# Layer 1's maximum subtracted by TensorE, a reordered first turn, and a store moved between loads, in a four-layer gated attention kernel

## Time and profile before

| what | value |
| --- | --- |
| median of the runs | 2130.57 us (2121.48, 2130.57, 2133.06) |
| the profiled execution, its own time | 2118.36 us |
| its span | 2116.6 us |
| granted TensorE clock, mean | 0.927 |
| PE busy | 1850.4 us, 87% |
| DVE busy | 1648.8 us, 78% |
| ACT busy | 583.1 us, 28% |
| POOL busy | 655.1 us, 31% |

### The profile page before, as it was taken

One profiled execution on the slowest core, in us unless ns is written; L12 is line 12 of the kernel. 1 busy time (PEld: TensorE's weight loads), 2 busy tenths in 40 slices (PEclk: granted clock), 3 DMA queues, 4 the chain that ended last, 5 costly groups with the idle time before them and its releaser, 6 DMA issues. The chain is left out here.

```text
span 2116.6 us, 37275 instructions
## 1 busy us (share of the span) xinstructions
PE 1850.4 (87%) x14832; PEld 1038.7 (49%) x14832; DVE 1648.8 (78%) x2940; ACT 583.1 (28%) x1331; POOL 655.1 (31%) x786
## 2 busy tenths in 40 slices
PE   8687879888798887988874799999999999999987
PEld 6333455435554355533542355555555555555543
DVE  4489776996669966699655688888888888888895
ACT  3321233212322123222234122222222222222344
POOL 3410223002330023300222543434344444444463
PEclk8899989998799987999877899999999999999998
DMA  8737204362043610446005211111111112111011
GB/s 238 209 122 212 77 2 137 109 191 65 2 141 116 184 60 2 141 120 180 1 1 174 80 51 51 51 51 50 51 51 46 51 35 66 26 46 31 26 41 51
DMA packets 141771, 176.48 MB, mean 83 GB/s; under 512 B 46752, under 2 KB 81728, under 8 KB 141472
## 3 DMA queue, kind: packets, MB, share of 16 engines
q1 hardware_dynamic: 139584, 172.88, 27.6%
q10 hardware_dynamic: 2016, 1.22, 0.3%
HBM read 131.98 MB, written 42.08 MB: 82 GB/s over the span
## 5 line engine op out<-in xcount | busy, mean ns | idle before, releaser
L1266 POOL TENSOR_TENSOR early_vare<-early_mv,w_eps 128x1 f32<-128x1 f32 x96 | 29.7, 309 | 750.2 <-DVE early_mv L1349 741.4
L2404 POOL TENSOR_TENSOR la_q<-la_straight,la_rot 128x512 f32<-128x512 f32 x128 | 163.0, 1274 | 163.7 <-DVE la_rot L2474 163.7
L434 PE MATMUL la_ps<-w_xTh,w_wqh 128*128 128x512 bf16 x512 | 196.2, 383 | 14.4 <-POOLq L116 8.0
L832 PE MATMUL early_ps<-early_products,w_heads 128*32 128x512 f32 x1024 | 140.1, 672 | 63.4 <-DVE early_products L1502 35.9
L435 PE MATMUL la_ps<-w_xTl,w_wqh 128*128 128x512 bf16 x512 | 195.0, 381 | 0.0
L436 PE MATMUL la_ps<-w_xTh,w_wql 128*128 128x512 bf16 x512 | 194.6, 380 | 0.0
L434 PE MATMUL la_ps<-w_woh,la_oTh 128*128 128x512 bf16 x512 | 194.0, 379 | 0.3 <-issue 0.3
L435 PE MATMUL la_ps<-w_wol,la_oTh 128*128 128x512 bf16 x512 | 194.0, 379 | 0.0
L436 PE MATMUL la_ps<-w_woh,la_oTl 128*128 128x512 bf16 x512 | 194.0, 379 | 0.0
L2417 POOL TENSOR_TENSOR la_p<-la_s,la_rec 128x256 f32<-128x256 f32 x128 | 89.9, 703 | 273.3 <-DVE la_rec L2495 273.3
L2336 ACT ACTIVATE la_oTh<-la_ps 128x256 bf16<-128x256 f32 x256 | 84.0, 380 | 293.5 <-PE la_ps L2219 293.5
(11 more groups left out here) (352 smaller groups left out, 4609.4 us busy)
## 6 DMA issues: line engine op xcount, KB each, us to landing
early_vR<-scr_v SPq DMA_DIRECT2D x128, 257.0 KB, 5.2
early_wkv<-wkv SPq DMA_DIRECT2D x32, 512.0 KB, 4.5
la_v<-v SPq DMA_DIRECT2D x64, 256.0 KB, 4.0
k<-early_ctxt SPq DMA_DIRECT2D x32, 256.0 KB, 3.9
v<-early_ctxt SPq DMA_DIRECT2D x64, 128.0 KB, 3.0
scr_p<-early_weights SPq DMA_DIRECT2D x16, 512.0 KB, 2.6
early_pR<-scr_p SPq DMA_DIRECT2D x32, 256.0 KB, 3.5
w_raw_q<-in_Wq SPq DMA_DIRECT2D x8, 1024.0 KB, 7.4
```

Of the source, the lines that this page charges most:

```text
L434: pe.matmul(out, lh[c], rh[c], start=(first and c == 0), stop=False)
L832: last = pe.matmul(out[32 * g:32 * g + 32, :], w["heads"][:, HEADS * (1 - odd):HEADS * (1 - odd) + 32], src(2 * g + odd), start=(opens and ...
L2404: rope_sum.send(pool.tensor_tensor(dst, straight[:, slot, :], rot[:, slot, :], ALU.add))
```

## The change

It has three parts.

1. The subtraction. `shift_scores` becomes `largest`: VectorE takes only the negated maximum. TensorE adds it to the scores in PSUM with a product of the identity and the maximum, repeated 16 times by a stride of zero (`centre`, two products a tile). ScalarE takes the exponential from PSUM into ee, half by half. `largest(3)` stands ahead of `times_values(1)`, and a second group of last-layer keys and values is ahead of the first `sum_depth`.
2. The store. Tile 3's eight value loads are issued four and four, with the store of its weights between.
3. The first turn. The opening's loads and products are in another order, Wq comes in two halves; the splits of the later weights, the signs, POOL's low splits, the stores of layer 1's values and ScalarE's splits 6 and 7 have other places.

```diff
     def load_product(self, sp):
-        sp.dma_start(self.wq[:, :, :], io["L0_Wq"].rearrange("(c p) n -> p c n", p=P)).then_inc(self.loaded, 16)
-        sp.dma_start(self.wk[:, :, :], io["L0_Wk"].rearrange("(c p) n -> p c n", p=P)).then_inc(self.loaded, 16)
-        sp.dma_start(self.bq[:, :], io["L0_bq"]).then_inc(self.loaded, 16)
-        sp.dma_start(self.bk[:, :], io["L0_bk"]).then_inc(self.loaded, 16)
+        sp.dma_start(self.bq[:, :], io["L0_bq"]).then_inc(self.wk_loaded, 16)
+        sp.dma_start(self.bk[:, :], io["L0_bk"]).then_inc(self.wk_loaded, 16)
+        sp.dma_start(self.wk[:, :, :], io["L0_Wk"].rearrange("(c p) n -> p c n", p=P)).then_inc(self.wk_loaded, 16)
+        for h in range(2):
+            cols = slice(2 * h * P, 2 * (h + 1) * P)
+            sp.dma_start(self.wq[:, :, cols], io["L0_Wq"].rearrange("(c p) n -> p c n", p=P)[:, :, cols])\
+              .then_inc(self.wq_loaded[h], 16)
...
     def product(self, pe, banks):
-        pe.wait_ge(self.loaded, 4 * 16)
-        for m in range(C):
-            banks.wait_free(pe, 0, "M", m)
...
+        pe.wait_ge(self.wk_loaded, 3 * 16)
         banks.wait_free(pe, 0, "r")
...
+        banks.wait_free(pe, 0, "s")
...
+        for m in range(C):
+            if m % 2 == 0:
+                pe.wait_ge(self.wq_loaded[m // 2], 16)
+            banks.wait_free(pe, 0, "M", m)
...
         banks.wait_free(pe, 0, "c")
...
-        banks.wait_free(pe, 0, "s")
```

On SP, first turn:

```diff
-                    first_keys_values(0, 1, 2, 3)
+                    first_keys_values(0, 1, 2)
...
                     if j == 1:
-                        for k in range(2):
-                            load_values(sp, turn, k)
+                        if turn == 0:
+                            first_keys_values(3)
+                        else:
+                            for k in range(2):
+                                load_values(sp, turn, k)
                 if turn == 0:
-                    first_keys_values(4, 5, 6, 7)
+                    first_keys_values(4, 5)
+                    load_values(sp, turn, 0)
                     for g in range(2):
+                        first_keys_values(KV - 2 + g)
                         prep.wait_kv_kept(sp, KV - 2 + g)
                         load_kv_weights(turn, g)
+                    load_values(sp, turn, 1)
```

On SP, every turn:

```diff
-                shifted_values(turn, 3)
-                weights_by_shift(turn, 3)
+                banks.wait_filled(sp, turn, "sum1", 1)
+                load_values(sp, turn, 3, range(CH // 2))
+                write_weights(turn, 3)
+                load_values(sp, turn, 3, range(CH // 2, CH))
+                read_weights(turn, 3)
```

On TensorE:

```diff
+                def centre(j):
+                    for h in range(2):
+                        mx1_ready.wait(pe, turn, 2 * j + h)
+                        at = slice(h * (TP // 2), (h + 1) * (TP // 2))
+                        centred.send(pe.matmul(banks.bank("dot1", j, h).rearrange("p (t w) -> p t w", w=WIN), ident,
+                                               mx1[:, at].unsqueeze(2).to_broadcast([P, TP // 2, WIN]),
+                                               start=False, stop=True, skip_group_check=True))
...
                 queries_keys(1)
-                last_keys_values(0)
+                last_keys_values(0, 1)
                 sum_depth(0)
                 queries_keys(2)
-                last_keys_values(1, 2)
+                centre(0)
+                last_keys_values(2)
                 sum_depth(1)
                 queries_keys(3)
+                centre(1)
                 last_keys_values(3, 4, 5)
                 sum_depth(2)
                 last_keys_values(6, 7)
                 sum_window(0)
                 out_proj(0)
+                centre(2)
                 last_keys_values(8, 9)
                 sum_depth(3)
-                last_keys_values(10, 11)
+                last_keys_values(10)
+                centre(3)
+                last_keys_values(11)
                 sum_window(1)
```

On ScalarE:

```diff
             def exponentials1(turn, j):
-                banks.wait_drained(act, turn, "dot1", j, 0)
-                banks.wait_drained(act, turn, "dot1", j, 1)
-                exp1_ready.send(act.activation(ee[:, :, :], ee[:, :, :], ACT.Exp, scale=float(CH) ** -0.5))
+                for h in range(2):
+                    at = slice(h * (TP // 2), (h + 1) * (TP // 2))
+                    if h == 0 and j >= 1:
+                        p1_ready.wait(act, turn, j - 1)
+                    centred.wait(act, turn, 2 * j + h)
+                    banks.drain(act.activation(ee[:, at, :].rearrange("p t w -> p (t w)"), banks.bank("dot1", j, h),
+                                               ACT.Exp, scale=float(CH) ** -0.5), "dot1", j, h)
...
                     aT_high.send(act.activation(aTh[:, j, :, :], aT[:, j % 2, :, :], ACT.Copy))
+                    if turn == 0 and j < 3:
+                        prep.high(act, *(("R1",), ("W1",), ("Wqd", "Wkv", "R3"))[j])
...
                 route_exp(turn, 0, e0, R0)
-                if turn == 0:
-                    prep.split_kv_high(act, 6)
                 hsT_copy(turn, 0)
                 if turn == 0:
-                    prep.split_kv_high(act, 7)
+                    prep.split_kv_high(act, 6, 7)
```

On POOL:

```diff
-                    prep.split_kv_low(pool, 0, 1, 2, 3)
+                    prep.split_kv_low(pool, 0, 1, 2)
+                rstd_of(turn, 1)
+                if turn == 0:
+                    prep.split_kv_low(pool, 3)
                     pool.wait_ge(prep.biased, 1)
-                rstd_of(turn, 1)
                 add_bias(turn, 0, 1)
                 if turn == 0:
-                    prep.split_kv_low(pool, 4, 5, 6, 7)
+                    prep.split_kv_low(pool, 4, 5)
                 rstd_of(turn, 2)
+                if turn == 0:
+                    prep.split_kv_low(pool, 6, 7)
```

On VectorE:

```diff
             def first_turn(j):
-                if j == 0:
+                if j == 1:
                     prep.low(dve, "R1")
-                elif j == 1:
+                elif j == 2:
                     prep.low(dve, "W1")
-                elif j == 2:
+                elif j == 3:
                     prep.low(dve, "Wqd", "Wkv", "R3")
-                else:
-                    prep.below_zero(dve)
-                    prep.signs(dve)
...
                 n = st.step(dve.tensor_scalar(rec[:, :], rec[:, :], w["gates"][:, 0:1], None, ALU.mult))
+                if turn == 0:
+                    prep.below_zero(dve)
+                    prep.signs(dve)
+                    dve.wait_ge(prep.signed, 2)
...
-                def shift_scores(j):
+                def largest(j):
...
-                        st.link(dve.tensor_reduce(mx1[:, at], dots, AX.X, ALU.max))
-                        ins = dve.tensor_tensor(ee[:, at, :], dots,
-                                                mx1[:, at].unsqueeze(2).to_broadcast([P, TP // 2, WIN]), ALU.subtract)
-                        banks.drain(ins, "dot1", j, h)
+                        mx1_ready.send(dve.tensor_reduce(mx1[:, at], dots, AX.X, ALU.max, negate=True))
...
                 times_keys(3)
                 divide(2)
+                largest(3)
                 times_values(1)
-                shift_scores(3)
                 divide(3)
```

More of the change, by code:

```diff
@@ L302, in product @@
         banks.fill(last, "r")
+        banks.wait_free(pe, 0, "s")
+        for c in range(C):
+            last = pe.matmul(banks.bank("s")[:, 0:1], bq[:, c:c + 1].to_broadcast([P, P]), bk[:, c:c + 1],
+                             start=(c == 0), stop=(c == C - 1))
+        banks.fill(last, "s")
+        for m in range(C):
+            if m % 2 == 0:
+                pe.wait_ge(self.wq_loaded[m // 2], 16)
+            banks.wait_free(pe, 0, "M", m)
+            for c in range(C):
+                last = pe.matmul(banks.bank("M", m), wq[:, c, m * P:(m + 1) * P], wk[:, c, :],
+                                 start=(c == 0), stop=(c == C - 1))
+            banks.fill(last, "M", m)
         banks.wait_free(pe, 0, "c")
@@ L308, in product @@
         banks.fill(last, "c")
-        banks.wait_free(pe, 0, "s")
-        for c in range(C):
-            last = pe.matmul(banks.bank("s")[:, 0:1], bq[:, c:c + 1].to_broadcast([P, P]), bk[:, c:c + 1],
-                             start=(c == 0), stop=(c == C - 1))
-        banks.fill(last, "s")
     def gate(self, act):
@@ L677, in attention1 @@
                     keep_kv(turn, f)
[L678 removed]
+                banks.wait_filled(sp, turn, "sum1", 0)
+                load_values(sp, turn, 2)
                 for f in range(8, 10):
@@ L1250, in _ @@
             ahead(0, None)
-            prep.high(act, "R1", "W1", "Wqd", "Wkv", "R3")
             prep.wait_direct(act)
```

65 lines of the change are left out of this document (32 added, 33 removed).

## The result

The changed kernel takes 2090.05 us (median of four runs, 2083.76 to 2094.82); the kernel before took 2127.2 us in its four runs beside them. The ratio is 0.984 (95% interval 0.981 to 0.987): 1.6% faster. The profiled execution fell from a span of 2116.6 to one of 2082.0 us, by 34.6. The forecast was 2096 us and a gain of 34.3.

What follows compares the result with a forecast made beforehand. TensorE bounds the last layer, VectorE layer 1's attention, and only waits early turn 0. Gains of 13.3 + 3.3 + 3 x 5.9 = 34.3 us from the 2130.6 median give 2096 us; own range 2087 to 2106, with rivals and run spread 2080 to 2114.

Steps and rivals of the forecast that it cites:

- 1 opening: Program start: earlier weight loads and product order r, s, M, c let the projections begin sooner; gain 3.7 us.
- 2 scores: Turn 0's first scores: sign steps and low splits move out of the way; gain 2.7 us, bounds 0 to 4.3.
- 3, 4 scratch and experts: Turn 0: values' stores and roots go earlier, gain 2.0 us (1 to 4); layer 0's experts start earlier, gain 9.15.
- 5 new wait: Turn 0, up to the second product pair: late splits 6 and 7 delay reloaded last-layer weights; loss 4.3 us.
- 6, 8 attention, turn 0: Turn 0's attention: subtraction on TensorE and the store between value loads, without a half-clocked sum; gain 3.3 us.
- 6, 7, 8 attention, turns 1 to 3: Attention: subtraction on TensorE, window sum at full clock, store between value loads; gain 5.9 us each turn.
- +1 for a slow start of M: Opening: r and s placed first may leave the clock low when M starts, costing 1 us.
- -5 if the clock costs nothing: Opening: best bound of its term, a gain of 5 us instead of 3.7.
- Part 4: Layer 0's experts in turn 0: ScalarE's hidden-state copies no longer stand behind split 6; gain 9.15 us.
- rival (c): Turn 0: GpSimd's splits 6 and 7 lose the port to VectorE's products; gain 30 or 26 us; chance 0.15.
- Part 7: Attention: sum_window(1)'s second half runs at full clock, 1.9 us instead of 3.5.
- rival (a): Attention gives only VectorE's 2 us a turn, as the read stays late and sum half-clocked; 2109 us; chance 0.18.

Runs made afterwards that it cites:

- e5: The kernel before, unchanged, profiled a second time; span 2123.5 us.
- e6: The changed kernel, unchanged, profiled a second time; span 2089.1 us.
- e11: The kernel before with e9's filler products on TensorE and nothing else; 2076.6 us, ratio 0.979.
- e12: The changed kernel with e9's filler products on TensorE and nothing else; 2051.1 us, ratio 0.967.
- e2: The changed kernel with the product M first again, then r, s and c, new loads kept; first bias addition at 45.4 us (44.5 in the changed kernel).
- e7: The kernel before with only the subtraction moved to TensorE and the keys' products that go with it; 2110.3 us, ratio 0.995.
- e3: The changed kernel with splits 6 and 7 of the last layer's weights back in their old places on GpSimd and ScalarE; ratio 0.980, span 2082.3 us.
- e1: The changed kernel with tile 3's weights stored after all eight value loads, as before the change; ratio 0.991, span 2101.9 us.
- e10: The changed kernel with the subtraction back on VectorE and the last layer's keys in their old order; ratio 0.993, span 2118.8 us.
- e8: The changed kernel with splits 6 and 7 early again and the second last-layer keys product behind the first depth sum again; 2079.3 us, ratio 0.981.
- e9: The kernel of e8 plus bf16 filler products, never read, in TensorE's waits in the second routed network and layer 2; 2046.55 us, ratio 0.966.

## Why the prediction was right, and where it wasn't

Three pairs of profiles measure each step: the first, e5 with e6, e11 with e12. Gains in us:

```
step                                  forecast   first    e5/e6   e11/e12   mean
1 opening                                3.7      1.2      2.9     -0.7      1.1
2 scores                                 2.7      2.1      2.3      1.9      2.1
3, 4 scratch and experts                11.15    11.2     12.8      8.3     10.8
5 new wait                              -4.3     -5.3     -5.7     -5.9     -5.6
6, 8 attention, turn 0                   3.3      2.65     4.7      3.3      3.5
6, 7, 8 attention, turns 1 to 3         17.7     13.9     16.7     17.7     16.1
sum                                     34.3     25.7     33.7     24.5     28.0
```

**Opening: the term was mis-sized, 3.7 for 1.1.** "r takes 4.1" was carried over from a place where the clock was up. At the head of the program it takes 7.0, in each of the nine profiles of the new order. The +1 for a slow start of M did not come, since M had started slowly before as well. The start at 7.4 and c at 4.1 were right, and the bound "-5 if the clock costs nothing" was the wrong end of the range. In e2, M did start 7 us earlier, and what came last paid instead. The size measured is not sharp: the first bias addition starts between 42.0 and 44.5 us in those nine profiles and between 43.0 and 45.8 in the four of the old order (before, e5, e7, e11), where c alone took from 5.1 to 7.0 us, by where the clock rose and fell.

**Scores, scratch, experts: right.** Part 4's wait went as worked out. Its cause was put half wrongly: the forecast set ScalarE's copies free by moving split 6 behind them, and e3 shows that 9 of the 11 us of this stretch come with the split in its old place. A new small wait, 1.75 us for split 5's load ahead of the routing, wasn't foreseen, and is inside the measured sum.

**The new wait: right in kind, 4.3 for 5.6.** The chain was as written: roots, splits, store, reload, two groups, two sums. What it left out is that TensorE, idle for 9.18 us, starts the groups at the lower clock: a granted clock of 0.50 and 0.61 us a product up to 117.5 us, then 0.99 and 0.38. Splits against products, rival (c), did meet at the port, on VectorE's side and for 3.7 us, but under the wait. And e3 shows the step needn't have been there: 22.5 us with the splits early.

**Attention: right in mechanism, over by 1.6 us of 17.7 on the mean.** In turn 2 of the first pair the stage gained 5.67 us for 5.9, the sum came 14.0 us ahead of the last products for 13.9, the wait for the read was 3.76 for 3.4, and a centring product took 0.95 us (30.5 us for 32 of them) for 0.93. Part 7 is borne out in every turn: the second half of sum_window(1) takes 1.9 us in turns 1 to 3 of the changed kernel, e1, e6 and e7, and 3.4 to 3.6 in those of before, e5 and e10, where VectorE subtracts; TensorE is idle for 0.5 us ahead of it instead of 2.1. Turn 1 gained only 3.6: its first depth sum ran at half clock and the first pair to the second took 13.0 us instead of 11.4. That is a loss on paper: ahead of it, the stretch from the first out0 addition to add_ffn(0) took 23.2 us instead of 24.6. The lower clock falls either here or there, in e5's kernel before as well (23.2 and 13.8). With the terms added as if they were independent the sum came out right, but they aren't: without the subtraction the store gives nothing (e10), and rival (a)'s worry, the read that stays late, is what e7 alone shows (7.3 us over three turns).

**What the forecast took for granted:** that layer 2 keeps its length. It lies behind every gain, and it is 62 to 71 us long depending on where its 0.8 to 2.7 us of TensorE's idle time fall against the clock. The first pair got 12.6 us from it, e5/e6 0.4 and e11/e12 -0.8. The last layer didn't quite keep its length either: from turn 3's last sign to the end 1004.4 us before and 1007.3 after (1008.0 and 1006.2 in e5 and e6).

So in the profile set beside the forecast's 34.3 us, it was right by two errors that met: the parts gave 8.6 us less than forecast, and layer 2 gave 12.6 that nobody counted, less 3.7 lost elsewhere. That agreement to 0.3 us is luck. In e5/e6 there was next to nothing to make up, 33.7 us from the parts; with the clock held the parts gave 24.5. The parts were over-counted by 0.6 to 9.8 us, 6 on the mean of three pairs. The medians point the same way, 37 us between the runs side by side and 25.5 with the clock held, each give or take 6, so by themselves they would not settle it.

One sum of the forecast is off: its own range, 2087 to 2106, is put down to the bounds of the opening and of part 5, and these reach from 2091 to 2105 only. It takes the bounds of parts 2 and 3 as well to come near 2087.

Left open: in turns 1 and 2 layer 2 took 70.7 or 70.8 us in five of six stretches where VectorE subtracts (before, e5, e10), 68.8 or 68.9 in the changed kernel's four (e6 among them), and 70.75 and 69.1 in e7. What decides between these two at the end of the attention wasn't tried; with the fillers the difference is gone. The run-to-run share of the clock in other stretches (23.2 or 24.6 us ahead of add_ffn, the last layer) is read from traces only.

## What to carry to other kernels

When a stretch that nobody edited has changed its length, look at its granted clock, and profile both kernels again before explaining anything by the edit. If TensorE idles a microsecond or two at a time on the path, products that nobody reads, placed inside those waits, can be worth more than the edit in hand: 32 to 44 us here, by the ratios of e8 and e9, changed and e12, before and e11. When a late transfer's queue position is mended, check whether work that was moved out of its way still needs to be; and when two edits touch one wait, price them together, in both orders.

## What the runs showed of the hardware

Equal instruction streams differ by 7 us in 69, with idle gaps of equal length, by where in them TensorE's granted clock falls (e6). Thirty-two one-column f32 products start 0.11 us apart and take 3.6 us where the clock stays up (e6's c), 0.21 us apart and 7.0 at half (r, in all nine profiles of the new order), so running them first costs some 3 us. Fillers that start 0.22 us apart, 208 in four turns in e9, show no cost where they lie in waits of 0.8 to 2.7 us: the stretches that hold them became shorter. A GpSimd subtraction of 2.19 us that starts first holds back both a VectorE product of two SBUF operands (10.67 us a pair for 8.76) and a one-input normalisation in f32 (2.33 for 0.55).
